# Two adaLN transformer layers on one core: where the float16 high halves are made, which slot follows the output product, and two pieces of the FFN walk

## The reference, cut to what matters

```python
h = _layernorm(x) * (1 + ca) + sa
x = x + ga * attention(h)          # layer 0 causal with a decay in the distance, layer 1 full
h = _layernorm(x) * (1 + cb) + sb
x = x + gb * ffn(h)                # layer 0: silu(h Wg) * (h Wu) * scales, then Wd (704 wide)
                                   # layer 1: 8 experts (176 wide), the top 2 of each token, and a shared FFN (352 wide)
```

## Time and profile before

| | |
|---|---|
| median of 3 runs | 1612.35 us (1607.53 to 1614.57) |
| profiled execution | 1610.37 us |
| its span, first to last instruction | 1608.7 us |
| TensorE busy | 1433.1 us (89%) |
| VectorE busy | 1203.9 us (75%) |
| ScalarE busy | 1037.8 us (65%) |
| GpSimd busy | 306.7 us (19%) |
| mean granted TensorE clock | 0.958 |

### The profile page before, as it was taken

How to read it: one execution, slowest core, us unless ns; L and a number is a source line. 1 busy time by engine, 2 the same in 40 slices (tenths; PEclk the granted TensorE clock), 3 DMA queues, 4 the chain that set the end, 5 groups by cost and what they waited for, 6 DMA issues and landing times.

```text
span 1608.7 us, 35116 instructions
## 1 busy us (share of the span) xinstructions
PE 1433.1 (89%) x13272; PEld 600.5 (37%) x13272; DVE 1203.9 (75%) x1592; ACT 1037.8 (65%) x2043; POOL 306.7 (19%) x367
## 2 busy tenths in 40 slices
PE   7877888899899989986899989998999899998987
PEld 5543333333333344442233333333333333245764
DVE  5577788788786034788899969996999689536665
ACT  2244566777688823321799978997999788953432
POOL 1201122000000022223500038002200120144134
PEclk9988899999999999997899999999999999999998
DMA  7621121111000002212200200000000000012453
GB/s 226 130 41 39 47 65 32 30 28 47 5 2 2 1 14 60 53 33 59 91 7 7 52 6 7 7 6 7 7 7 7 7 2 2 20 54 90 142 158 105
DMA packets 57610, 68.53 MB, mean 43 GB/s; under 512 B 10563, under 2 KB 53123, under 8 KB 56707
## 3 DMA queue, kind: packets, MB, share of 16 engines
q1 hardware_dynamic: 54379, 57.90, 13.6%
q0 software_dynamic: 3072, 8.39, 1.7%
HBM read 45.29 MB, written 26.74 MB: 45 GB/s over the span
## 4 chain that ended last, share of the span: by engine, by line
issue 28%; PE 18%; POOL 7%; DVE 6%; ACT 3%; DMA 1%; another core or an unknown queue 0%; SPq 0%; ACTq 0%; POOLq 0%; DVEq 0%
DVE mpart L1670 5%; PE psum L1251 3%; PE psum L1297 2%; PE psum L1226 2%; PE psum L1183 2%; ACT probs L1421 2%; PE psum L1316 2%; PE psum L1235 2%; PE psum L1158 1%; PE psum L1288 1%; PE psum L1127 1%; POOL ffn_w L909 1%; POOL key_region L921 1%; POOL key_region L923 1%; DMA key_region<-in_w_up 1%
## 5 line engine op out<-in xcount | busy, mean ns | idle before, releaser
L1670 DVE TENSOR_REDUCE mpart<-psum 128x2 f32<-128x1024 f32 (+2 forms) x832 | 914.9, 1157 | 120.9 <-PE psum L1127 94.0
L1421 ACT ACTIVATE probs<-psum 128x512 f32<-128x512 f32 (+3 forms) x1664 | 846.8, 573 | 191.8 <-PE psum L1158 112.3
L1183 PE MATMUL psum<-probs,v_region 128*17 128x256 f32 (+2 forms) x6144 | 500.8, 399 | 11.4 <-ACT out_sb L1436 7.6
L1127 PE MATMUL psum<-key_region,row_region 50*128 50x512 f16 (+3 forms) x1664 | 320.7, 381 | 72.8 <-DVE mpart L1670 56.5
L1158 PE MATMUL psum<-row_region,key_region 52*128 52x512 f16 (+3 forms) x1664 | 351.2, 383 | 17.9 <-ACT probs L1421 15.4
L1158 PEld LDWEIGHTS psum<-row_region,key_region 52*128 52x128 f16 x1664 | 96.5, 93 | 372.2 <-ACT probs L1421 297.8
L1183 PEld LDWEIGHTS psum<-probs,v_region 128*17 128x17 f32 x6144 | 103.0, 96 | 209.6 <-issue 112.6
L1127 PEld LDWEIGHTS psum<-key_region,row_region 50*128 50x128 f16 x1664 | 94.5, 94 | 168.4 <-DVE mpart L1670 103.5
L871 POOL TENSOR_SCALAR vare<-mv 128x4 f32<-128x4 f32 x16 | 3.7, 230 | 642.7 <-DVE mv L1591 640.0
L1456 ACT ACTIVATE probs<-psum,gate_s 128x512 f32<-128x512 f32 (+1 forms) x24 | 16.5, 688 | 75.7 <-PE psum L1226 75.7
L974 POOL TENSOR_TENSOR key_region<-probs,key_region 128x512 f16<-128x512 f32 (+1 forms) x24 | 27.9, 1165 | 179.9 <-ACT key_region L1465 179.8
(11 more groups left out here) (179 smaller groups left out, 1331.4 us busy)
## 6 DMA issues: line engine op xcount, KB each, us to landing
parts<-key_region SPq DMA_DIRECT2D x32, 256.0 KB, 3.3
key_region<-parts SPq DMA_DIRECT2D x48, 128.0 KB, 4.3
row_region<-parts SPq DMA_DIRECT2D x192, 32.0 KB
sorted_x<-in_zero SPq DMA_DIRECT2D x46, 128.0 KB, 2.6
key_region<-sorted_x SPq DMA_DIRECT2D x46, 128.0 KB
sorted_y<-key_region SPq DMA_DIRECT2D x46, 128.0 KB
key_region<-in_wmod SPq DMA_DIRECT2D x2, 1536.0 KB, 12.6
x_sb<-in_x SPq DMA_DIRECT2D x4, 512.0 KB, 8.7
```

Of the source, the lines that this page charges most:

```text
L1127: mm = pe.matmul(bank(b + par)[:, 0:w], rows[at, g, hp, r * P:(r + 1) * P], keys[at, g * HP + hp, q * CH:q * CH + w], start=True, stop=not ...
L1183: mm = pe.matmul(psum[32 * h:32 * h + VW, SUM_BANK, lo:hi], v_sb[:, jt, g * HG + h, :], probs[:, (S0[y] + s) % 2, h, lo:hi], start=(jt == ...
L1421: nc.scalar.activation(probs[:, (S0[y] + s) % 2, 2 * hp + par, off:CH], psum[:, e % 3, off:CH], ACT.Exp, scale=SCALES[y]).then_inc(s_p, 1)
L1670: V.tensor_reduce(mpart[:, n % NG, at:at + 2, q:q + 1], psum[:, b:b + 2, 0:w], AX.X, ALU.max).then_inc(drained(*item)[0], 1)
```

## The change

There are four edits.

1. The item "ln" of every norm but the first is split. "ln" now holds the transposes and the float32 copy, and drains the slot with it. A new item "lh" makes the high half from the float32 copy in SBUF, and raises `s_high`; GpSimd's low half belongs to "lh". In attention "lh" stands one step (k = 7) behind "ln" (k = 6); elsewhere it stands right behind "ln". Waits for the last "hid" or for "v" go to "lh".
2. At an "op" the turn of the slot family is set back to the slot of that product, so the block behind it takes the other slot, whatever stood between "oq" and "op".
3. ln(1,3) moves from behind piece 5 of chunk 0 to behind piece 1 of chunk 1.
4. At the end of layer 0's FFN one max block goes ahead of the projection of rows of chunk 2, and nm(2,3) goes between its "qk" and its "ql".

```diff
@@ attention_walk
                 if k == 6:
                     out.append(("ln", 2 * y + 1, i))
+                if k == 7:
+                    out.append(("lh", 2 * y + 1, i))
@@ ffn0_walk
     for c in range(NC[0]):
-        out.extend(hidden_pair(0, 0, c) + tail(0, c))
+        out.extend(hidden_pair(0, 0, c) + (tail(0, c) if c < 5 else []))
...
+            if tc == 1 and c == 1:
+                out.extend(tail(0, 5))
             if c == 2:
                 out.append(("nm", 2, p))
...
-    project_rows(p - 1, 1)
-    out.append(("nm", 2, p))
-    out.append(("v", 1, p - 1))
-    out.append(("ln", 2, p))
+    blocks(1)
+    out += [("qk", 1, p - 1, 0), ("nm", 2, p), ("ql", 1, p - 1, 0), ("v", 1, p - 1), ("ln", 2, p)]
@@ new
+def with_high_features(items):
+    out = []
+    for it in items:
+        out.append(it)
+        if it[0] == "ln" and it[1] and ("lh", *it[1:]) not in items:
+            out.append(("lh", *it[1:]))
+    return out
@@ slots
+                elif item[0] == "op":
+                    family = slot_family(n, ("oq", *item[1:]))
+                    turn[family] = family.index(slot[own][0])
@@ split_of
-            return s_low, [it for it in walk if it[0] == "ln" and it[1]].index(("ln", q, tc)) + 1
+            return s_low, nth["lh", q, tc]
@@ low_features, GpSimd
-                pool.wait_ge(*drained(*item))
+                pool.wait_ge(s_high, nth[item])
@@ project, TensorE
-                    pe.wait_ge(*drained("ln", 2, tc))
+                    pe.wait_ge(s_high, nth["lh", 2, tc])
@@ ln, ScalarE
-                if q % 2:
-                    act.wait_ge(*filled("v", y, tc))
-                elif q == 2:
-                    act.wait_ge(*filled(*last_hid(tc)))
                 act.wait_ge(*filled(*item))
...
-                    for dst in (mod_t[xh_buf(q, tc)], hT16[tc][:, 0, :, :]):
+                dst = mod_t[xh_buf(q, tc)] if q else hT32[:, tc, :, :]
...
+            def high_features(item):
+                q, tc = item[1:]
+                act.wait_ge(*drained("ln", q, tc))
+                act.wait_ge(*(filled("v", q // 2, tc) if q % 2 else filled(*last_hid(tc))))
+                for c in range(KD):
+                    ins = nc.scalar.activation(hT16[tc][:, 0, c, :], mod_t[xh_buf(q, tc)][:, c, :], ACT.Identity)
+                ins.then_inc(s_high, 1)
```

More of the change, by code:

```diff
@@ L389, in with_halves @@
     return out
+def with_high_features(items):
[5 more added lines that the diff above has]
+    return out
 def stages():
     middle, done = ffn0_walk()
-    middle = with_halves(middle)
+    middle = with_high_features(with_halves(middle))
     first, tiles, rest = ffn1_walk()
@@ L397, in stages @@
             [("load", 1)] + middle + [("wo", 1)] + [("xb", 1, tc) for tc in range(NCH)],
-            attention_walk(1, done), with_halves(first), tiles, with_halves(rest)]
+            attention_walk(1, done), with_high_features(with_halves(first)), tiles, with_halves(rest)]
 IN_SLOT = ("mc", "mg", "mr", "ln", "qk", "v", "max", "mt", "ft", "bt", "oq", "hg", "dm", "dn", "lg", "px", "tx", "gu", "th", "dw")
@@ L590, in adaln_two_layers @@
         s_wdown = [sem(f"down_weights_loaded{y}") for y in range(NLAY)]
+        s_high = sem("features_high_ready")
         s_low = sem("features_split")
@@ L997, in _ @@
                     split_down(it[1])
-                elif it[0] == "ln" and it[1]:
+                elif it[0] == "lh":
                     low_features(it)
@@ L1383, in ln @@
                 act.wait_ge(s_modc, y + 1)
-                if q % 2:
-                    act.wait_ge(*filled("v", y, tc))
-                elif q == 2:
-                    act.wait_ge(*filled(*last_hid(tc)))
                 act.wait_ge(*filled(*item))
-                if q == 0:
-                    for c in range(KD):
-                        ins = nc.scalar.activation(hT32[:, tc, c, :], bank(b + c), ACT.Identity,
-                                                   bias=modc[:, y, c:c + 1], scale=modc[:, y, c + 2:c + 3])
-                else:
-                    for dst in (mod_t[xh_buf(q, tc)], hT16[tc][:, 0, :, :]):
-                        for c in range(KD):
-                            i = 4 * (q % 2) + c
-                            ins = nc.scalar.activation(dst[:, c, :], bank(b + c), ACT.Identity,
-                                                       bias=modc[:, y, i:i + 1], scale=modc[:, y, i + 2:i + 3])
-                ins.then_inc(drained(*item)[0], 1)
+                dst = mod_t[xh_buf(q, tc)] if q else hT32[:, tc, :, :]
+                for c in range(KD):
+                    i = 4 * (q % 2) + c
+                    ins = nc.scalar.activation(dst[:, c, :], bank(b + c), ACT.Identity,
+                                               bias=modc[:, y, i:i + 1], scale=modc[:, y, i + 2:i + 3])
+                ins.then_inc(drained(*item)[0], 1)
+            def high_features(item):
+                q, tc = item[1:]
+                act.wait_ge(*drained("ln", q, tc))
+                act.wait_ge(*(filled("v", q // 2, tc) if q % 2 else filled(*last_hid(tc))))
+                for c in range(KD):
+                    ins = nc.scalar.activation(hT16[tc][:, 0, c, :], mod_t[xh_buf(q, tc)][:, c, :], ACT.Identity)
+                ins.then_inc(s_high, 1)
             def high_parts(item):
@@ L1500, in _ @@
                     ln(it)
+                elif it[0] == "lh":
+                    high_features(it)
                 elif it[0] == "qk":
```

## The result

The changed kernel took 1592.03 us (median of 7 runs, 1586.55 to 1595.17), the kernel before on the same chip 1607.07 us (7 runs). The ratio is 0.9891, 95% interval [0.9864, 0.9919]: 15 us less, where 14.9 were forecast. The difference came out; how it is made up did not, as the rows show. The time itself lies 5.5 us under the 1597.5 us that the prediction named: it counted from a median of three runs, 1612.35 us, and over seven runs the kernel before comes to 1607.07.

What follows compares the result with a forecast made beforehand. No single engine bounds the kernel: TensorE, ScalarE and VectorE run as one ring, so TensorE's stalls count as kernel time. Terms 4.8 + 2.7 + 1.8 + 5.1 + 0.5 = 14.9 us off 1612.35 gave 1597.5 us, range 1590 to 1610.

Steps and rivals of the forecast that it cites:

- The step that failed: Layer 0's FFN: normed tiles take 1.4 us, so TensorE newly waits 1.3 to 1.5 us before ln(2,0).
- part 3: Layer 0's FFN, ln(1,3) moved back: down product gains 7.6 us, 1.0 and 1.5 given back, net 5.1 us.
- The second half of the step: Layer 0's FFN: with a shorter wait the clock stays up through the first down product, 2.5 us gained.
- part 1: Attention chunk ends, high halves a step later: 4.8 us at four ends, 2.7 us at layer 0's first two.
- alike chunk end: One in layer 0, three in layer 1, each with a 2.03 us wait: 1.2 us gain each, between 0.7 and 1.7.
- Part 2: Layer 0's three chunk ends, block behind "op" takes the other slot: 1.8 us, bounds 0.8 and 3.1.
- Part 4: End of layer 0's FFN, nm(2,3) ahead of "ql": 0.3 us; shorter copies of ln(3,3) give another 0.2.
- A: Rival, whole kernel: the clock falls as before whatever is done; gain 10.4 us, 1602 us; chance 0.2.
- B: Rival: TensorE's waits were covered, VectorE's reductions could be the real pace; about 1607.5 us; chance 0.18.
- C: Rival, attention chunk ends: second burst costs as much as the first, kernel 10 us slower, 1622 us; chance 0.07.
- D: Rival: the change doesn't do what it says; taken as true for layer 1's slots; no chance given.

Runs made afterwards that it cites:

- e10: Changed kernel with ln(1,3) right ahead of the first down product, behind the first pair of chunk 1, second measurement: 1583.34 us, ratio 0.984 to the kernel before.
- e2: Changed kernel without the slot's turn set back at "op": 1601.81 us, ratio 0.9895 to the kernel before.
- e1: Changed kernel with the high halves right behind "ln" again in attention, still read from SBUF: 1609.28 us, ratio 0.9958 to the kernel before.
- e4: Changed kernel with ln(1,3) right ahead of the first down product, behind the first pair of chunk 1: 1591.68 us, ratio 0.9851 to the kernel before.
- e9: Changed kernel measured a third time, no edit: 1593.77 us, ratio 0.991 to the kernel before.
- e8: Kernel before with only the slot's turn set back at "op": 1608.77 us, ratio 0.9987 to the kernel before.
- e5: Changed kernel measured again, no edit: 1591.52 us, ratio 0.9902 to the kernel before.
- e7: Changed kernel with two more Identity copies ahead of the high halves in attention: 1606.38 us, ratio 0.999 to the kernel before.

## Why the prediction was right, and where it was wrong

The direction and the total were right, 14.9 us of forecast against 15.0. Two terms of the sum were not, with opposite signs, so the total was partly luck. The named time, 1597.5 us, was 5.5 too high, because the median of three runs under it was 5.3 above that of seven.

**The step that failed: what part 3 gives back.** "low halves 2.3, normed tiles 1.4 ... then waits 1.3 to 1.5 us before ln(2,0)". The 1.4 us were taken from the earlier trace rows, where GpSimd is quiet. Here nm(2,0) runs beside GpSimd's two low halves of the hidden chunk (591.58 to 593.89) and takes 2.96 us; VectorE's four in the changed kernel, with their shortest, median and longest in ns:

```profile
L1625 DVE TENSOR_SCALAR attn_region<-x_sb,mv,rstd x4: 401/776/1236, 591.7 to 594.3; 128x256 f32<-128x256 f32 x4
```

and in e10, where GpSimd is busy beside only the first:

```profile
L1625 DVE TENSOR_SCALAR attn_region<-x_sb,mv,rstd x4: 398/399/568, 594.0 to 595.1; 128x256 f32<-128x256 f32 x4
```

Two tiles of 0.4 us took 1.15 and 1.24, each of them begun while GpSimd was at work and ended 0.15 us after GpSimd's instruction (591.58 to 592.74, then 592.69 to 593.89); the two behind them took 0.4 again. The price stood in the kernel before as well, right ahead of the 1.94 us wait of the earlier trace rows, and I passed over it:

```profile
577.65 3.05 DVE L1607 TENSOR_SCALAR attn_region<-x_sb,mv,rstd 128x256 f32<-128x256 f32 x4 [0.50 <-POOL rstd L874]
...
577.59 1.16 POOL L974 TENSOR_TENSOR key_region<-probs,key_region 128x512 f16<-128x512 f32 x1
578.92 1.30 POOL L974 TENSOR_TENSOR key_region<-probs,key_region 128x512 f16<-128x512 f32 x1 [0.18 <-ACT key_region L1465]
```

The Trainium skill, "SBUF — State Buffer", section "Who interferes with whom", has a rule that these rows agree with: a tensor_scalar of VectorE in its two-port mode and a GpSimd operation take turns at one pair of ports, each for a whole instruction. That these tiles run in that mode no row shows by itself. My sum had both engines in one line of additions and never asked what ran beside. It was 1.56 us short there (2.96 instead of 1.4), the wait became 3.11, and so of the 5.84 us of waits at that place (1.94 and 3.90) 0.94 were saved.

The second half of the step, "so I take the 2.5 us too", failed as well. I took the clock's fall at the down product as a matter of how long the wait before it is. The changed kernel's windows show the clock through the 3.11 us wait:

```profile
588.00:592.00 4.00, 3.72 (x18) 1.47 (x15) 1.02 (x2) 3.54 (x7) 2.78 (x4) 1.00 0.01 2
592.00:596.00 4.00, 1.17 (x10) 1.07 (x11) 3.35 (x5) 0.01 (x1) 1.89 (x2) 1.00 0.00 0
```

It stayed at 1.00, with TensorE busy 1.17 of 4 us. Behind the same wait in e2 it fell, and the transposes took 1.94 us instead of 1.06:

```profile
609.21 1.94 PE L1078 MATMUL psum<-ident,attn_region 128*128 128x128 f32 x8 [3.10 <-DVE attn_region L1621]
```

It also fell after 2.03 us in the earlier trace rows, and after 2.86 in one of the two executions above. The Trainium skill, "TensorE: Matmul & The Clock Gate", "Part 1: The HAM clock gate", has the chip look at free-running moments; the two pairs of executions agree with it. So one fall more or less can't be forecast here, and I had counted on it. What the runs show is a mean: with less and shorter waiting the time at the lower clock is 18 to 22 us less. Part 3's 5.1 us came to 0.94 of waits, which is within the error of zero.

**The term that was too small: part 1.** Forecast 7.5; the step's move alone measured 9 to 10, and 1.7 us of waits that e1 saves too come on top. The mechanism was right: the first wait 0.67 (forecast 0.7). The second was 0.41, forecast 0.9: I laid Exps, copies and Exps end to end, 3.3 us from the first Exp to the end of the copies, where ScalarE takes 2.95 (941.42 to 944.37), because each pair of groups overlaps by about 0.15. And I took 1.2 of a possible 1.7 for each alike chunk end because the clock might fall as before. In the profile they gave more: 2.4, 2.0 and 4.8 us in layer 1, the last since the fall behind the third end's router product, 10 us of low time in all before, is absent too (in e4 and e9 one of these falls is back and the end takes 55.2, not 53.8). The waits at these four ends fell by 3.86 us together; at the first two of layer 0, 2.06 became 1.16 and 0.37, 2.22 became 1.05 and 0.34, 1.36 us in all, where 2.7 was forecast for them. Waits therefore give about half (5.2 us seen to go, of them 3.5 by the move), the clock the rest.

**Part 2** was forecast at 1.8 and measured 2.2 to 2.5, inside its bounds. The waits for the addition went from 0.95, 1.07 and 1.06 to 0.74, 0.85 and none (1.49). Of the waits behind them two got shorter, 0.90 to 0.71 and 2.06 to 1.68, and one longer, 0.25 to 0.41: 0.4 us, 1.9 in all. One more wait of the kernel before, at the third chunk end of layer 0, is gone in the changed kernel, but in e2 as well, where part 2 is undone; the first row is of the kernel before, the second of e2:

```profile
418.00 1.09 PE L1065 MATMUL psum<-ident,attn_region 128*128 128x128 f32 x8 [0.97 <-DVE mpart L1670]
...
425.23 1.09 PE L1078 MATMUL psum<-ident,attn_region 128*128 128x128 f32 x8
```

In both kernels without that wait the clock had fallen ahead of it (0.50 from 406 to 412 us in the changed kernel), so TensorE came later. It is no gain of part 2. That at the first two ends a second block needs the slot of "op" after all was right: 0.21 and 0.22 us gained there, forecast 0.4.

**Part 4**, 0.3 us, as forecast: from the last matmul of the down product ahead of ln(2,3) to the transposes 7.08 us, before 7.38. No experiment isolates it.

**The sum again.** At zero the waits seen to go are 5.2 + 1.9 + 0.9 + 0.3 = 8.3 us; the fit has 8.2 to 9.8 for the changed kernel. The clock gave 18 to 22 us less low time, 6.3 to 7.7 us at the slope. Together that is 15 to 16. Part by part it is less well known: 9 to 10 for the move and 1.7 for the rest of part 1, then 2.3, 0 and 0.3, make 13 to 14 of the 15 us, and what is left is within the error of each comparison.

**The rivals.** A, the clock falls as before: no; low time fell from 135 us (142 on one chip) to 113–117, and at the first two chunk ends of layer 1 the profiles with a wait of 2.03 us (before, e8) have a fall behind each, those of the changed kernel (its first, e5, e9) none. B, the waits were covered: no, the waits that went sum to 8.3 us, and at zero the time is 8.2 to 9.8 us less. The argument against B, that VectorE is idle in every one of the waits, was read too strongly: it is busy 0.39 of the 2.03 us ahead of 953.56, and 0.89 of the 0.95 us in the earlier trace rows, with the addition itself. C did not happen, but e7 shows it real: a wait of 1.45 us behind the moved copies took the whole gain. That it starts at 1.3 us no run shows. D, that it doesn't do what it says, held for layer 1's slots, as priced.

## What to carry to other kernels

Where two engines pass banks back and forth, a long burst on one is worth cutting in two with the partner's work between; finer cuts won nothing here. When work is moved, look up what each other engine does at the new place, not only what its own engine does: a duration read where GpSimd is quiet does not hold beside it, and the same four tiles took 1.37 and 3.05 us in the one trace that I had. And before moving a piece far, try the gap just ahead of the product that was waiting: there it filled a wait and its followers fell under a long product.

## What the runs showed of the hardware

- VectorE's tile of 128x256 float32 from SBUF to SBUF, 0.40 us, takes 1.15 to 1.32 us when it meets nearly the whole of a GpSimd subtraction of 128x512 (1.15 to 1.30 us). Four tiles take 1.37 us alone, 2.28 beside one such instruction and 2.96 to 3.05 beside two, in the changed kernel and in the one before.
- With TensorE busy 89% of the time, a us at the lower clock costs 0.35 us of kernel time, over 146 runs; the changed kernel's own runs differ in the time at that clock by 6 to 13 us (standard deviation, in three groups of 6 or 7), and that makes most of their spread.
- The stage of expert tiles takes 110.6 to 112.3 us in eight of the 14 profiles and 114.9 to 118.0 in six, with 0 to 5 us at the lower clock. The six are all four of the first chip of the experiments (e1 to e4), e8 and the kernel before. The kernel before is also 5.5 us longer at zero on that first chip than on the other two. So it goes at least partly with the chip. e8 and the profile of the kernel before leave open whether a part goes with the change; e4 and e10, one kernel on two chips, are 14.1 and 13.1 us under the kernel before at zero, which speaks against it. The cause is open.
